# Queries projected once from packed weights and doubled when they leave PSUM, with two of four stacks and an output bias moved into the first batch

## The chip, the cores and the metric

The kernel runs on one core of a Trainium2 chip. The metric is device time in microseconds: the median of three executions was 816.04 us (814.54 to 821.61). All operands are float32. A product that needs full precision is made in one of two ways: as a plain float32 matmul, or as three matmuls on operands split into a rounded high part and a remainder (`_hi`, `_lo`, type float32r).

## The reference, cut to what matters

x is (8, 64, 256), so 512 tokens, and the context is (8, 1024, 256). Six layers follow each other, each of them `x = x + layer(layernorm(x))`. The change touches the first one only:

```python
q = split_heads(query @ w_q.T + b_q)          # query = layernorm(x); 16 heads of 16
k = split_heads(key @ w_k.T + b_k)            # key = value = ctx_1024
v = split_heads(value @ w_v.T + b_v)
scores = jnp.einsum('bhqd,bhkd->bhqk', q, k) / scale
attn = jax.nn.softmax(scores, axis=-1)
ctx = jnp.einsum('bhqk,bhkd->bhqd', attn, v)
out = ctx.transpose(0, 2, 1, 3).reshape(B, -1, D_MODEL) @ w_o.T + b_o
```

After it come an S4 filter over the batch axis, a mixture of 16 experts, a masked attention on the same context, a state-space layer, and a mixture of 9 experts.

## The kernel before, in words

Each engine has its own stream of instructions, written by hand in `build`; the streams meet only at semaphores. An engine runs its stream strictly in order, so a wait in it holds up everything behind it.

**The first layer.** The normalized tokens are transposed into `xnT` (features on partitions). Queries are kept in four stacks g = 0 to 3 of 64 features (`STACKS`). To make up for the split of the keys into a high and a low half, which share the 128 partitions of `k_stack`, every query feature must stand twice, on partitions 0 to 63 and again on 64 to 127. Before the change this doubling is done on the host: `wq` in the tile `first` has each group of 64 columns twice (512 columns per half of the input), and `bq` likewise. TensorE makes four products of 128 x 512 (L1882), ScalarE adds the bias and rounds each into `q_hi` (L1019), VectorE makes the remainder `q_lo` (L1315), and GpSimd spreads both over four masked copies for one batch element, `q_stack_hi` and `q_stack_lo` (`split_heads`, L633, one pair of operations for each stack).

**Batches.** Eight batch elements follow, `batch(b, ...)` on TensorE, ScalarE and VectorE, each of eight steps i. Step i takes the scores of two heads-groups (stack g = i // 2) against 1024 keys, and beside them makes one piece of keys or values: pieces of this batch's second half of the keys at i = 0 and 2, values at i = 1, 3, 5, 7, and at i = 4 and 6 the first half of the keys of the **next** batch element. VectorE takes the maximum of the scores (L1376, L1379), and then copies out the piece (`key_piece` L1324, `value_piece` L1335) and the first half of the previous step's transposed probabilities (L1348). ScalarE takes the exponential (L995), the high parts of keys (L982), the other half of the transposes (L1008), and at i = 1 the high part of the next context, `ctx_hi` (L974). GpSimd makes the low part, `ctx_lo` (`context_low`, L650, two operations of 128 x 1024). TensorE may start a key piece of the next batch only when both of those are done: `pe.wait_ge(ctx_lo_ready, DC * b + DC)` in `project_keys`.

**GpSimd's stream.** It is written out at L800 to L829, and near the change it reads:

```python
context_low(0, 0, range(1))
split_heads(0)
taps_parts = filter_taps()
next(taps_parts)
context_low(1, 1)
diagonals(0, 0)
split_heads(1)
```

`filter_taps` is a generator that holds the arithmetic of the S4 filter, cut in parts that are placed between the work of the attention. Its first part is 13 small operations (L660, the tiles `s_wr` to `s_g`).

**PSUM.** Before the change the queries use banks 2, 3, 5 and 6 (`Q_BANKS`), and the first two key pieces banks 4 and 7 (`FIRST_BANKS`). Bank 7 later holds the weighted values (`weigh`).

Of the kernel before, what the change touches and what calls it, by code (L numbers as in the profile page):

```python
# [20 lines left out]
P = 128  # L21
# [35 lines left out]
SPLIT1_AT = {GROUPS * m + g: 3 * (m - 1) + (g - 1) // 2 for m in (1, 2) for g in (1, 3, 5)}  # L57
LAYERS = 6

Q_BANKS, FIRST_BANKS = (2, 3, 5, 6), (4, 7)  # L60

# [49 lines left out]
def part(tile, layout, name):  # L113
    a, b = layout[name]
    return tile[:, a:b]
# [29 lines left out]
def build(nc, d, out):  # L145
    ctx = ExitStack()
    with ctx:
# [11 lines left out]
        def sb(region, name, shape, dt=F32):  # L159
            width = int(np.prod(shape[1:])) * 4  # L160
            at = place[region]
            place[region] = at + -(-width // 64) * 64
            assert place[region] <= ends[region], (name, region, place[region] - ends[region])
            return nc.alloc_sbuf_tensor_at(name, shape, dt, offset=at)
# [36 lines left out]
        w_kv = [[sb("phase", f"w_{n}_{part_of}", [P, DC, D], F32R) for part_of in ("hi", "lo")] for n in "kv"]  # L201
        k_stack = sb("phase", "k_stack", [P, STACKS, KEYS], F32R)
        V = sb("phase", "V", [P, KC, D])
        probs = [sb("phase", f"probs{k}", [P, KEYS]) for k in range(2)]
        probsT = [sb("phase", f"probsT{k}", [P, KC, PAIRS, P]) for k in range(DC)]
        q_part = [sb("phase", f"q_{n}", [P, STACKS, TOK], F32R) for n in ("hi", "lo")]
# [174 lines left out]
        def pb(i):  # L381
            return banks[:, i, :] if isinstance(i, int) else banks[:, bass.ds(i, 1), :].rearrange("p a n -> p (a n)")
# [43 lines left out]
        w2_hi_ready, w2_lo_ready, w2_before = w_hi_ready, w_lo_ready, 2 - 2 * PLAIN  # L426
        share_ready, spread_ready, spread_turned, spreadT_ready = inverted, diag_ready, spread_taken, masked_ready
        share_before = DC * B
        last_taken, last_before = q_done, STACKS
        up_done, gelu_done, down_done = sem("up_done"), sem("gelu_done"), sem("down_done")  # L430

        mask_loaded = sem("mask_loaded")
# [59 lines left out]
        def norm_of(k, t):  # L492

            return TC * (k - 1) + t + 1
# [462 lines left out]
        def _(act):  # L957
# [56 lines left out]
                    .then_inc(w_hi_ready, 1)  # L1014
            transposed(1)
            context_high(0, 0)
            for g in range(STACKS):
                act.wait_ge(q_done, g + 1)
                nc.scalar.activation(q_part[0][:, g, :], pb(Q_BANKS[g]), ACT.Identity, bias=part(first, FIRST, "bq")[:, g:g + 1])\  # L1019
                    .then_inc(q_hi_ready, 1)  # L1020
            for half in range(2):
                key_piece(half + 1, 0, half, FIRST_BANKS[half])

            act.wait_ge(loaded["later"], 16)
            nc.scalar.activation(s4dt[:], part(later, LATER, "log_dt"), ACT.Exp).then_inc(s4_exp, 1)
# [236 lines left out]
        def _(dve):  # L1262
# [41 lines left out]

            dve.wait_ge(loaded["x"], 16)
            layer_norm(1)
            transposed(1)

            dve.wait_ge(ctx_hi_ready, DC)
            nc.vector.tensor_tensor(ctx_lo[0][:, 1, :], ctx_raw[:, 1, :], ctx_hi[0][:, 1, :].bitcast(F32), ALU.subtract).then_inc(ctx_lo_ready, 1)  # L1310
            bq, bk, bv = part(first, FIRST, "bq"), part(first, FIRST, "bk"), part(rows, ROWS, "bv")
            dve.wait_ge(loaded["first"], 16)
            for g in range(STACKS):
                dve.wait_ge(q_hi_ready, g + 1)
                nc.vector.scalar_tensor_tensor(q_part[1][:, g, :], pb(Q_BANKS[g]), bq[:, g:g + 1], q_part[0][:, g, :].bitcast(F32),  # L1315
                                               ALU.add, ALU.subtract).then_inc(q_lo_ready, 1)

            def key_piece(k_piece, c, half, bank=4):

# [52 lines left out]
            def batch(b, par, last, tile=None):  # L1372
                later_one = not (isinstance(b, int) and b == 0)
                for i in range(8):
                    dve.wait_ge(scores_done, 8 * b + (i + 1))
                    nc.vector.tensor_reduce(negmax_raw[i % 2][:], two(i % 2),  # L1376
                                            AX.X, ALU.max, negate=True).then_inc(raw_max, 1)
                    dve.wait_ge(raw_max, 8 * b + (i + 1))
                    nc.vector.tensor_scalar(negmax[i % 2][:], negmax_raw[i % 2][:], 0.25, None, ALU.mult)\  # L1379
                        .then_inc(max_ready, 1)  # L1380
                    if i in KEYS_AT:
                        key_piece(4 * b + 3 + KEYS_AT.index(i), 1, KEYS_AT.index(i))
                    elif i in VALUES_AT:
                        value_piece(piece_at(b, i, last), b, VALUES_AT.index(i))
                    elif i in NEXT_KEYS_AT and not last:
                        key_piece(4 * b + 5 + NEXT_KEYS_AT.index(i), 0, NEXT_KEYS_AT.index(i))
                    if i == 5 and tile is not None:
                        add_tile(tile)
                    if i == 4:
                        invert_sums(b, 0)  # L1390
                    if i == 0 and later_one:
                        invert_sums(b - 1, 1)
                    if i == 0 and later_one:
                        gather(b - 1, 1 - par, 0)
                    if i == 4 and later_one:
                        gather(b - 1, 1 - par, 1)
                    if i >= 1:
                        first_half(b, i - 1)
                    elif later_one:
                        first_half(b - 1, 7)  # L1400

                    if last and 1 <= i < TC:
                        dve.wait_ge(tile_added, i + 1)
                        norm_begin(2, i - 1)
                    if last and 5 <= i < TC + 4:
                        norm_tile(2, i - 5)
# [1 line left out]
            for half in range(2):  # L1408
                key_piece(half + 1, 0, half, FIRST_BANKS[half])
            dve.wait_ge(loaded["rows"], 16)  # L1410
            dve.wait_ge(xn_ready, norm_of(1, TC - 1))
            nc.vector.tensor_tensor(X[:], X[:], over(part(rows, ROWS, "bo"), TC, 1), ALU.add).then_inc(tile_added, 1)
            batch(0, 0, False)
            dve.wait_ge(s4_norm, 1)
            nc.vector.reciprocal(s4g[2][:], s4g[2][:]).then_inc(s4_norm, 1)
# [436 lines left out]
        def _(pe):  # L1852
# [23 lines left out]
            transpose_tokens(1)  # L1876
            keep_running(4, 1, table[:, 0:512])
            pe.wait_ge(loaded["first"], 16)
            wq = weights(first, FIRST, "wq", DC)
            pe.wait_ge(xt0_ready, 1)  # L1880
            pe.wait_ge(xt1_ready, 1)
            for g in range(STACKS):  # L1882
                for i in range(DC):
                    last = mm(pb(Q_BANKS[g]), wq[:, i, g * P:(g + 1) * P], xnT[:, i, :], i == 0, i == DC - 1)
                last.then_inc(q_done, 1)

            def three(o, a, b):
# [37 lines left out]
            def weigh(b, c, q):  # L1925

                pe.wait_ge(piece_taken, piece_at(b, VALUES_AT[q], isinstance(b, int) and b == B - 1))
                if q == 0:  # L1930
                    pe.wait_ge(pt0_ready, 8 * b + PAIRS * (c + 1))
                    pe.wait_ge(pt1_ready, 8 * b + PAIRS * (c + 1))
                    pe.wait_ge(diag_ready, DC * b + (c + 1))
                    if not (isinstance(b, int) and b == 0 and c == 0):
                        pe.wait_ge(masked_ready, DC * b + c)

                    for j in range(PAIRS):
                        mm(pb(7)[PAIR_W * j:PAIR_W * (j + 1), P:2 * P], part(table, TABLE, "pick"), inv_diag[:, j, :], True, True)
                for kc in (2 * q, 2 * q + 1):
                    for j in range(PAIRS):  # L1940
                        at = c * P + PAIR_W * j
                        last = mm(pb(7)[PAIR_W * j:PAIR_W * (j + 1), 0:P], V[:, kc, at:at + PAIR_W],
                                  probsT[c][:, kc, j, :], kc == 0, kc == KC - 1)
                last.then_inc(quarter_done, 1)
# [572 lines left out]
```

## Time and profile before

| what | value |
|---|---|
| median of three executions | 816.04 us |
| the profiled execution, its own time | 815.67 us |
| its span from first to last instruction | 813.8 us |
| TensorE busy | 719.9 us, 88% of the span |
| VectorE busy | 585.6 us, 72% |
| GpSimd busy | 430.5 us, 53% |
| ScalarE busy | 417.8 us, 51% |
| mean granted TensorE clock | 0.968 of full |

An engine's busy share is a mean over six very different layers; the change lies in the first 60 us, so that part has to be read by itself. In the timelines a row is a group of instructions that follow each other: its start, its length, and in brackets how long the engine was idle before it and what ended that idle time. PE is TensorE, DVE VectorE, ACT ScalarE, POOL GpSimd. A float32 matmul stands in the trace as two instructions.

### The profile page before, as it was taken

Reading aid. Unit: us, or ns where it says so; the run is one execution under the profiler, and the core shown is the slowest. Engines: PE = TensorE matmul, PEld = TensorE weight load, DVE = VectorE, ACT = ScalarE, POOL = GpSimd, SP = SyncE. Lnnn points to the kernel's source line nnn. Section 1 sums busy time; section 2 is a strip of 40 time slices with the busy share of each in tenths; the row PEclk is TensorE's granted clock in tenths of the full one; section 3 lists DMA queues with packets and bytes.
Section 4 is the critical chain, followed back from the end, with each engine's and each line's share of the span. In section 5 each row is a group of like instructions: output and inputs, shape, how many; then the busy total and the mean of one; then the engine's idle time right before and its main releaser. Section 6 shows DMA issues by size and latency. Waiting matters only on the chain.

```text
span 813.8 us, 14674 instructions
## 1 busy us (share of the span) xinstructions
PE 719.9 (88%) x5252; PEld 562.6 (69%) x5252; DVE 585.6 (72%) x1210; ACT 417.8 (51%) x777; POOL 430.5 (53%) x417
## 2 busy tenths in 40 slices
PE   7899999999999997699999999999887776776886
PEld 3677777777777786599999999985463222222676
DVE  4788777887877857307777777715564999998585
ACT  3666656665665533146666666532337554432331
POOL 4637344363542712657878777556122879864130
PEclk9999999999999997899999999999999789989999
DMA  8011010010102049598989989988533700001000
GB/s 341 25 47 54 2 53 27 24 52 0 52 0 98 7 178 412 210 362 323 420 324 343 341 336 344 341 325 352 207 117 139 297 0 0 1 0 39 1 0 27
DMA packets 21225, 126.60 MB, mean 156 GB/s; under 512 B 2304, under 2 KB 6800, under 8 KB 13872
## 3 DMA queue, kind: packets, MB, share of 16 engines
q1 hardware_dynamic: 18288, 118.00, 38.3%
q0 software_dynamic: 2880, 7.87, 2.6%
q8 instruction: 32, 0.52, 0.3%
q14 instruction: 25, 0.20, 0.1%
HBM read 115.04 MB, written 10.81 MB: 155 GB/s over the span
## 4 chain that ended last, share of the span: by engine, by line
PE 57%; DVE 17%; POOL 10%; issue 8%; ACT 5%; DMA 2%; DVEq 0%; SPq 0%; ACTq 0%; POOLq 0%; PEldq 0%
PE banks L1854 51%; DVE banks L1760 6%; PE banks L1921 4%; DVE k_stack L1324 3%; POOL inject L924 3%; POOL y_rows L878 2%; ACT k_stack L982 1%; DVE negmax_raw L1376 1%; ACT ctx_hi L974 1%; DMA first<-in_first 1%; POOL f_lo L944 1%; DMA y_slots<-y_tile 1%; POOL rstd L622 1%; DVE shown L1770 1%; PE banks L2089 1%
## 5 line engine op out<-in xcount | busy, mean ns | idle before, releaser
L1854 PE MATMUL banks<-xT,raw 128*128 128x128 f32 x992 | 150.9, 275 | 2.3 <-issue 0.9
L1854 PEld LDWEIGHTS banks<-xT,raw 128*128 128x128 f32 x992 | 134.4, 191 | 6.1 <-issue 2.7
L858 POOL TENSOR_TENSOR w_lo<-raw,w_hi 128x1024 fp32r<-128x1024 f32 x48 | 113.2, 2379 | 1.9 <-ACT w_hi L1067 1.0
L1854 PE MATMUL banks<-shown,table 128*128 128x512 f32 x128 | 72.5, 697 | 42.2 <-DVE shown L1770 35.5
L995 ACT ACTIVATE probs<-banks,negmax 128x1024 f32<-128x1024 f32 x64 | 71.4, 1116 | 58.6 <-DVE negmax L1379 57.9
L924 POOL TENSOR_TENSOR inject<-BCbc,drive 128x1024 f32<-128x1024 f32 x32 | 75.0, 2352 | 36.4 <-DVE banks L1760 21.0
L1098 ACT ACTIVATE banks<-banks,later 128x128 f32<-128x128 f32 x192 | 65.2, 340 | 53.5 <-PE banks L1854 52.3
L1376 DVE TENSOR_REDUCE negmax_raw<-banks 128x1 f32<-128x1024 f32 x64 | 78.0, 1219 | 19.6 <-PE banks L1854 19.5
L1854 PEld LDWEIGHTS banks<-shown,table 128*128 128x128 f32 x128 | 24.6, 212 | 86.5 <-DVE shown L1770 67.6
L1588 DVE CAST mid_hi<-banks 128x128 fp32r<-128x128 f32 x192 | 55.5, 289 | 32.9 <-ACT banks L1098 30.6
L1760 DVE TENSOR_TENSOR_SCAN banks<-banks,inject 128x1024 f32<-128x1024 f32 x32 | 73.2, 2288 | 3.3 <-POOL inject L924 3.3
L1210 ACT ACTIVATE banks<-delta,exp_a 128x512 f32<-128x512 f32 x64 | 41.6, 682 | 62.2 <-DVE shown L1770 61.6
L1921 PE MATMUL banks<-table,probs 128*128 128x128 f32 x512 | 70.1, 280 | 0.0
L1854 PE MATMUL banks<-w_hi,mid_hi 128*128 128x256 f32 x192 | 69.7, 363 | 0.0
L982 ACT ACTIVATE k_stack<-banks,first 64x512 fp32r<-64x512 f32 x64 | 43.6, 681 | 42.8 <-PE banks L1854 41.9
L643 POOL TENSOR_TENSOR inv_diag<-table,inv_sums 128x512 f32<-128x512 f32 x16 | 16.6, 1040 | 91.4 <-DVE inv_sums L1342 54.9
L1324 DVE SCALAR_TENSOR_TENSOR k_stack<-banks,first,k_stack 64x512 fp32r<-64x512 f32 x64 | 48.0, 750 | 23.4 <-ACT k_stack L982 22.9
L1921 PEld LDWEIGHTS banks<-table,probs 128*128 128x128 f32 x512 | 55.9, 142 | 11.9 <-issue 11.3
L1590 DVE TENSOR_TENSOR mid_lo<-banks,mid_hi 128x128 fp32r<-128x128 f32 x192 | 56.0, 292 | 6.6
L1854 PE MATMUL banks<-k_stack,q_stack_hi 128*128 128x512 f32 x128 | 55.9, 436 | 0.0
L1854 PE MATMUL banks<-w_hi,mid_lo 128*128 128x256 f32 x192 | 54.0, 281 | 0.0
L1854 PE MATMUL banks<-w_lo,mid_hi 128*128 128x256 f32 x192 | 54.0, 281 | 0.0
(315 smaller groups left out, 1753.8 us busy)
## 6 DMA issues: line engine op xcount, KB each, us to landing
raw<-in_w SPq DMA_DIRECT2D x31, 2048.0 KB, 8.5
ctx_raw<-in_ctxT SPq DMA_DIRECT2D x8, 1024.0 KB, 4.8
ctxT<-in_ctxT SPq DMA_DIRECT2D x4, 2048.0 KB, 12.1
ctxN<-in_ctxN SPq DMA_DIRECT2D x4, 2048.0 KB, 12.4
BCbc<-bc_rows SPq DMA_DIRECT2D x6, 1024.0 KB, 14.2
x_slots<-zero SPq DMA_DIRECT2D x1, 3968.0 KB, 12.1
y_slots<-y_tile POOLq DMA_DIRECT2D x28, 128.0 KB, 6.9
wf<-in_w SPq DMA_DIRECT2D x9, 384.0 KB, 5.8
```

The costliest lines, as they stand in the source:

```text
L858: nc.gpsimd.tensor_tensor(w2_lo[i % WB][:, cols], raw[i % WB][:, EW // 2:][:, cols], w2_hi[i % 2][:, cols].bitcast(F32), ALU.subtract).the ...
L924: nc.gpsimd.tensor_tensor(inject[g % 2][:], Bbc[:, GS * g:GS * (g + 1), :], over(drive[:, m, :], GS, 1), ALU.mult).then_inc(inject_ready, 1)
L982: nc.scalar.activation(k_stack[at, DC * c + g, half * 512:(half + 1) * 512], pb(bank)[at, :], ACT.Identity, bias=part(first, FIRST, "bk")[ ...
L995: nc.scalar.activation(probs[i % 2][:], two(i % 2), ACT.Exp, bias=negmax[i % 2][:], scale=0.25, accum_out=sums[i // PAIRS][:, i % PAIRS:i ...
L1098: nc.scalar.activation(to, held, ACT.Gelu, bias=b1[:, bass.ds(at + u, 1)]).then_inc(gelu_done, 1)
L1324: last = nc.vector.scalar_tensor_tensor(k_stack[to, DC * c + g, cols], pb(bank)[at, :], bk[at, c:c + 1], k_stack[at, DC * c + g, cols].bit ...
L1376: nc.vector.tensor_reduce(negmax_raw[i % 2][:], two(i % 2), AX.X, ALU.max, negate=True).then_inc(raw_max, 1)
L1588: nc.vector.tensor_copy(mid_hi[n % HB][:], held).then_inc(mid_hi_ready, 1)
L1590: nc.vector.tensor_tensor(mid_lo[n % HB][:], held, mid_hi[n % HB][:].bitcast(F32), ALU.subtract).then_inc(mid_lo_ready, 1)
L1760: nc.vector.tensor_tensor_scan(held, held, inject[g % 2][:].rearrange("p g n -> p (g n)"), 0.0, ALU.mult, ALU.add).then_inc(scanned, 1)
L1854: return nc.tensor.matmul(o, lhsT, rhs, start=start, stop=stop)
L1921: last = nc.tensor.transpose(pb(5 + half)[:, k * P:(k + 1) * P], probs[i % 2][:, kc * P:(kc + 1) * P], ident)
```

## The change

- VectorE packs `wq` into a new tile `wq_dense` without the doubled columns (one copy, between the layer norm and its copy of `xnT`), and TensorE multiplies from it: two products of 128 x 512 in place of four. `Q_BANKS` is now (2, 7) and `FIRST_BANKS` (4, 3).
- The doubling happens as the queries leave PSUM: for each stack ScalarE makes two operations on 64 partitions (`query_high`), and VectorE two (`query_low`).
- Stacks 0 and 1 (`EARLY_Q`) are taken where all four were taken before. On ScalarE stacks 2 and 3 come behind the first two key pieces. On VectorE stack 2 comes in step 1 and stack 3 in step 2 of the first batch.
- The output bias, one addition to `X` on VectorE ahead of the first batch, now lies in step 3 of the first batch.
- `weigh` of the first batch also waits for all four `q_lo`, since bank 7 held queries. GpSimd's stream has the same instructions in the same order.

```diff
-Q_BANKS, FIRST_BANKS = (2, 3, 5, 6), (4, 7)
+Q_BANKS, FIRST_BANKS = (2, 7), (4, 3)
+EARLY_Q = 2
...
+        wq_dense = nc.alloc_sbuf_tensor_at("wq_dense", [P, DC, D], F32, offset=place["phase"])
...
-            for g in range(STACKS):
-                act.wait_ge(q_done, g + 1)
-                nc.scalar.activation(q_part[0][:, g, :], pb(Q_BANKS[g]), ACT.Identity, bias=part(first, FIRST, "bq")[:, g:g + 1])\
-                    .then_inc(q_hi_ready, 1)
+            bq = part(first, FIRST, "bq")
+
+            def query_high(g):
+                c, at = g // 2, slice(64 * (g % 2), 64 * (g % 2) + 64)
+                act.wait_ge(q_done, c + 1)
+                for z in range(2):
+                    last = nc.scalar.activation(q_part[0][64 * z:64 * z + 64, g, :], pb(Q_BANKS[c])[at, :], ACT.Identity, bias=bq[at, g:g + 1])
+                last.then_inc(q_hi_ready, 1)
+
+            for g in range(EARLY_Q):
+                query_high(g)
             for half in range(2):
                 key_piece(half + 1, 0, half, FIRST_BANKS[half])
+            for g in range(EARLY_Q, STACKS):
+                query_high(g)
...
             layer_norm(1)
+            dve.wait_ge(loaded["first"], 16)
+            order.mark(nc.vector.tensor_copy(wq_dense[:].rearrange("p c (g n) -> p c g n", g=STACKS),
+                                             part(first, FIRST, "wq").rearrange("p (c g n) -> p c g n", c=DC, g=STACKS)[:, :, :, 0:64]))
             transposed(1)
...
-            for g in range(STACKS):
+
+            def query_low(g):
+                c, at = g // 2, slice(64 * (g % 2), 64 * (g % 2) + 64)
                 dve.wait_ge(q_hi_ready, g + 1)
-                nc.vector.scalar_tensor_tensor(q_part[1][:, g, :], pb(Q_BANKS[g]), bq[:, g:g + 1], q_part[0][:, g, :].bitcast(F32),
-                                               ALU.add, ALU.subtract).then_inc(q_lo_ready, 1)
+                for z in range(2):
+                    last = nc.vector.scalar_tensor_tensor(q_part[1][64 * z:64 * z + 64, g, :], pb(Q_BANKS[c])[at, :], bq[at, g:g + 1],
+                                                          q_part[0][at, g, :].bitcast(F32), ALU.add, ALU.subtract)
+                last.then_inc(q_lo_ready, 1)
...
+                    if not later_one and 0 < i <= STACKS - EARLY_Q:
+                        query_low(EARLY_Q + i - 1)
+                    if not later_one and i == STACKS - EARLY_Q + 1:
+                        add_out_bias()
...
             dve.wait_ge(loaded["rows"], 16)
-            dve.wait_ge(xn_ready, norm_of(1, TC - 1))
-            nc.vector.tensor_tensor(X[:], X[:], over(part(rows, ROWS, "bo"), TC, 1), ALU.add).then_inc(tile_added, 1)
             batch(0, 0, False)
...
-            wq = weights(first, FIRST, "wq", DC)
+            pe.wait_ge(dve_step, 1)
             pe.wait_ge(xt0_ready, 1)
             pe.wait_ge(xt1_ready, 1)
-            for g in range(STACKS):
+            for c in range(DC):
                 for i in range(DC):
-                    last = mm(pb(Q_BANKS[g]), wq[:, i, g * P:(g + 1) * P], xnT[:, i, :], i == 0, i == DC - 1)
+                    last = mm(pb(Q_BANKS[c]), wq_dense[:, i, c * P:(c + 1) * P], xnT[:, i, :], i == 0, i == DC - 1)
                 last.then_inc(q_done, 1)
...
-                    if not (isinstance(b, int) and b == 0 and c == 0):
+                    if isinstance(b, int) and b == 0 and c == 0:
+                        pe.wait_ge(q_lo_ready, STACKS)
+                    else:
                         pe.wait_ge(masked_ready, DC * b + c)
```

VectorE's stream before, from the queries' low parts to step 2 of the first batch (a name's trailing number tells buffers apart, "waits" names the semaphores):

```order
L1315 SCALAR_TENSOR_TENSOR q_lo<-banks,first,q_hi 128x512 [waits q_hi_ready,loaded_first]
L1315 SCALAR_TENSOR_TENSOR q_lo<-banks,first,q_hi 128x512 [waits q_hi_ready] x3
L1324 SCALAR_TENSOR_TENSOR k_stack<-banks,first,k_stack 64x512 [waits k_hi_ready] x4
L1412 TENSOR_TENSOR X<-X,rows 128x1024 [waits xn_ready,loaded_rows]
L1376 TENSOR_REDUCE negmax_raw_88<-banks 128x1 [waits scores_done]
...
L1335 TENSOR_TENSOR V<-banks,rows 128x512 [waits proj_done]
L1348 COPY probsT_82<-banks 128x4x128 [waits t_done]
L1376 TENSOR_REDUCE negmax_raw_88<-banks 128x1 [waits scores_done]
L1379 TENSOR_SCALAR negmax_90<-negmax_raw_88 128x1 [waits raw_max]
L1324 SCALAR_TENSOR_TENSOR k_stack<-banks,first,k_stack 64x512 [waits k_hi_ready] x2
L1348 COPY probsT_82<-banks 128x4x128 [waits t_done]
```

The same stretch of VectorE's stream now:

```order
L1332 SCALAR_TENSOR_TENSOR q_lo<-banks,first,q_hi 64x512 [waits q_hi_ready,loaded_first]
...
L1349 SCALAR_TENSOR_TENSOR k_stack<-banks,first,k_stack 64x512 [waits k_hi_ready] x4
L1401 TENSOR_REDUCE negmax_raw_89<-banks 128x1 [waits scores_done]
...
L1360 TENSOR_TENSOR V<-banks,rows 128x512 [waits proj_done]
L1332 SCALAR_TENSOR_TENSOR q_lo<-banks,first,q_hi 64x512 [waits q_hi_ready]
L1332 SCALAR_TENSOR_TENSOR q_lo<-banks,first,q_hi 64x512
L1373 COPY probsT_83<-banks 128x4x128 [waits t_done]
...
L1349 SCALAR_TENSOR_TENSOR k_stack<-banks,first,k_stack 64x512 [waits k_hi_ready] x2
L1332 SCALAR_TENSOR_TENSOR q_lo<-banks,first,q_hi 64x512 [waits q_hi_ready]
L1332 SCALAR_TENSOR_TENSOR q_lo<-banks,first,q_hi 64x512
L1373 COPY probsT_83<-banks 128x4x128 [waits t_done]
```

Four operations on `q_lo` stand ahead of the first key pieces, two behind the values of step 1, two behind the key piece of step 2; the addition to `X` is gone from ahead of the first maximum.

GpSimd's stream now, which differs from before in its line numbers alone, from the third stack of `split_heads(0)` to the next context's low part:

```order
L635 TENSOR_TENSOR q_stack_hi<-q_hi,table 128x256 [waits q_lo_ready]
L635 TENSOR_TENSOR q_stack_lo<-q_lo,table 128x256
L635 TENSOR_TENSOR q_stack_hi<-q_hi,table 128x256 [waits q_lo_ready]
L635 TENSOR_TENSOR q_stack_lo<-q_lo,table 128x256
L662 TENSOR_TENSOR s_wr<-s_ew,s_dt 128x32 [waits loaded_later,s4_exp]
...
L662 TENSOR_TENSOR s_g_107<-s_g_107,s_g_108 128x160 [waits pool_step]
L652 TENSOR_TENSOR ctx_lo_72<-ctx_raw,ctx_hi_71 128x1024 [waits pool_step,ctx_hi_ready]
L652 TENSOR_TENSOR ctx_lo_72<-ctx_raw,ctx_hi_71 128x1024 [waits ctx_hi_ready]
```

Nothing moved here, but the second wait for `q_lo_ready` in it is for an operation that VectorE now issues in step 2 of the first batch.

## Rows read from the trace of the kernel before

**Rows 1.** The page: busy time by engine, and the chain's shares by engine
```profile
PE 719.9 (88%) x5252; PEld 562.6 (69%) x5252; DVE 585.6 (72%) x1210; ACT 417.8 (51%) x777; POOL 430.5 (53%) x417
PE 57%; DVE 17%; POOL 10%; issue 8%; ACT 5%; DMA 2%; DVEq 0%; SPq 0%; ACTq 0%; POOLq 0%; PEldq 0%
```

**Rows 2.** The chain of work in order of time, first 76 us: start, length, what
```profile
1.79 7.89 DMA first<-in_first
...
11.43 8.51 PE banks L1854 x22
...
41.84 0.69 ACT k_stack L982
...
68.59 4.75 POOL ctx_lo L650 x2
73.47 2.23 PE banks L1854 x22
```

**Rows 3.** Timeline of PE, 10 to 62 us
```profile
11.43 7.10 PE L1854 MATMUL banks<-xnT,first 128*128 128x512 f32 x16 [0.56 <-ACT xnT L960]
17.98 0.80 PE L1854 MATMUL banks<-ctx_hi,w_k_hi 128*128 128x512 f32 x1
...
28.10 0.39 PE L1854 MATMUL banks<-w_v_hi,ctx_hi 128*128 128x256 f32 x1 [2.13 <-DVE k_stack L1324]
...
31.98 0.47 PE L1854 MATMUL banks<-k_stack,q_stack_hi 128*128 128x512 f32 x1
...
36.92 0.39 PE L1854 MATMUL banks<-w_v_hi,ctx_hi 128*128 128x256 f32 x1 [0.59 <-DVE k_stack L1324]
...
39.26 0.47 PE L1854 MATMUL banks<-k_stack,q_stack_hi 128*128 128x512 f32 x1
...
40.26 0.39 PE L1854 MATMUL banks<-ctx_hi,w_k_hi 128*128 128x512 f32 x1
```

**Rows 4.** Windows: busy us (instructions) of PE, PEld, DVE, ACT, POOL, granted clock, DMA
```profile
29.00:30.00 1.00, 1.00 (x7) 1.00 (x7) 0.46 (x2) 0.48 (x1) 0.84 (x3) 0.50 0.00 0
```

**Rows 5.** Timeline of DVE, 8 to 42 us
```profile
9.21 0.69 DVE L1296 COPY xnT<-banks 128x512 f32<-128x512 f32 x1 [0.78 <-PE banks L1868]
14.26 2.54 DVE L1310 TENSOR_TENSOR ctx_lo<-ctx_raw,ctx_hi 128x1024 fp32r<-128x1024 f32 x1 [4.37 <-ACT ctx_hi L974]
...
20.68 3.06 DVE L1324 SCALAR_TENSOR_TENSOR k_stack<-banks,first,k_stack 64x512 fp32r<-64x512 f32 x4 [0.63 <-ACT k_stack L982]
23.77 1.23 DVE L1412 TENSOR_TENSOR X<-X,rows 128x1024 f32<-128x1024 f32 x1
...
30.87 0.69 DVE L1335 TENSOR_TENSOR V<-banks,rows 128x512 f32<-128x512 f32 x1 [1.38 <-PE banks L1854]
...
35.36 1.51 DVE L1324 SCALAR_TENSOR_TENSOR k_stack<-banks,first,k_stack 64x512 fp32r<-64x512 f32 x2 [0.75 <-ACT k_stack L982]
```

**Rows 6.** Timeline of ACT, 8 to 36 us
```profile
10.76 0.58 ACT L960 ACTIVATE xnT<-banks 128x512 f32<-128x512 f32 x1
...
19.97 2.81 ACT L982 ACTIVATE k_stack<-banks,first 64x512 fp32r<-64x512 f32 x4 [0.70 <-PE banks L1854]
...
34.65 1.38 ACT L982 ACTIVATE k_stack<-banks,first 64x512 fp32r<-64x512 f32 x2
```

**Rows 7.** Timeline of POOL, 20 to 39 us
```profile
21.54 0.61 POOL L633 TENSOR_TENSOR q_stack_lo<-q_lo,table 128x256 fp32r<-128x256 f32 x1
23.20 0.24 POOL L660 TENSOR_TENSOR s_wr<-s_ew,s_dt 128x32 f32<-128x32 f32 x1 [1.05 <-ACT s_ew L1026]
...
23.84 1.48 POOL L660 TENSOR_TENSOR s_g<-s_wr,table 128x160 f32<-128x160 f32 x1
25.39 0.46 POOL L660 TENSOR_TENSOR s_g<-s_wi,table 128x160 f32<-128x160 f32 x1
...
30.32 0.52 POOL L660 TENSOR_TENSOR s_g<-s_g,s_g 128x160 f32<-128x160 f32 x1
33.89 4.74 POOL L650 TENSOR_TENSOR ctx_lo<-ctx_raw,ctx_hi 128x1024 fp32r<-128x1024 f32 x2 [3.04 <-ACT ctx_hi L974]
```

More of the change, by code:

```diff
@@ L428, in build @@
         share_before = DC * B
-        last_taken, last_before = q_done, STACKS
+        last_taken, last_before = q_done, DC
         up_done, gelu_done, down_done = sem("up_done"), sem("gelu_done"), sem("down_done")
@@ L1312, in _, with add_out_bias @@
             dve.wait_ge(loaded["first"], 16)
-            for g in range(STACKS):
+            def query_low(g):
+                c, at = g // 2, slice(64 * (g % 2), 64 * (g % 2) + 64)
                 dve.wait_ge(q_hi_ready, g + 1)
-                nc.vector.scalar_tensor_tensor(q_part[1][:, g, :], pb(Q_BANKS[g]), bq[:, g:g + 1], q_part[0][:, g, :].bitcast(F32),
-                                               ALU.add, ALU.subtract).then_inc(q_lo_ready, 1)
+                for z in range(2):
+                    last = nc.vector.scalar_tensor_tensor(q_part[1][64 * z:64 * z + 64, g, :], pb(Q_BANKS[c])[at, :], bq[at, g:g + 1],
+                                                          q_part[0][at, g, :].bitcast(F32), ALU.add, ALU.subtract)
+                last.then_inc(q_lo_ready, 1)
+            def add_out_bias():
+                dve.wait_ge(xn_ready, norm_of(1, TC - 1))
+                nc.vector.tensor_tensor(X[:], X[:], over(part(rows, ROWS, "bo"), TC, 1), ALU.add).then_inc(tile_added, 1)
+            for g in range(EARLY_Q):
+                query_low(g)
             def key_piece(k_piece, c, half, bank=4):
```

## The prediction

> **What bounds the kernel now.** I read the page first. TensorE is busy 88% of the span and VectorE 72% [rows 1], but that is a mean over six layers, and the change touches 60 us. So the second view is the chain of waits in order of time. In the first 76 us it runs from a transfer over TensorE's queries to the high and low copies of the keys and back, and then over GpSimd: `ctx_lo` holds TensorE up at 73.47 [rows 2]. The reader should see two things. The key piece of the next batch element, whose copy by ScalarE stands at 41.84, is on the chain; and GpSimd, busy only 53% of the time, is on it wherever `ctx_lo` comes late. The third view is the timeline of each engine, 8 to 42 us, from which I rebuild the schedule.
>
> TensorE's queries take 7.10 us for 16 instructions, and the first keys follow at 17.98, though `ctx_lo` had been ready since 16.80 [rows 3, 5]. That is the delay the change aims at. GpSimd, in its own stream, finishes the fourth stack of query copies at 22.15, does the first part of the filter from 23.20 to 30.84, waits 3.04 us, and makes the next context's low part from 33.89 to 38.63 [rows 7]. TensorE first needs that at 40.26 [rows 3], in step 4 of the first batch. Slack: 1.63 us. This small number decides the case.
>
> **The change, part by part.**
>
> *Packing.* `first` lands at 1.79 + 7.89 = 9.68 [rows 2]. A copy of 128 x 512 costs at most the 0.69 us of the `xnT` copy [rows 5], at least nothing. VectorE's `xnT` then ends by 9.68 + 0.69 + 0.69 = 11.06, and ScalarE's half ends at 11.34 [rows 6], so TensorE still starts at 11.43. Price 0, cover 0.28 us, and the worst case costs less than that again.
>
> *Queries on TensorE.* Eight instructions for 16: 3.55 us less, done at 14.98. The keys now wait for `ctx_lo`, 16.80, and start about 16.9: gain 1.08 of the 3.55 us.
>
> *Copies, lead-in.* A key copy of 64 x 512 is the nearest row: 3.06 / 4 = 0.765 us on VectorE, 2.81 / 4 = 0.70 us on ScalarE [rows 5, 6]. Half the partitions save nothing against 0.69 us for 128 x 512. ScalarE fits the two early stacks (2.8 us from 14.13) in before the first keys are ready, 19.97 - 1.08 = 18.89. VectorE goes from 16.80 over four low parts to 19.86 and over four key copies to 22.92, where it was 23.74: 0.82 us gained. Taking away the addition to `X` (1.23 us at 23.77) gains nothing here, as it lay under TensorE's first scores.
>
> *ScalarE behind the keys.* 18.89 + 2.81 + 4 x 0.70 for stacks 2 and 3 = 24.50; two small exponentials (0.34) and the next key copies (2 x 0.70) end at 26.24. VectorE's last copy of that piece then ends at 27.22 against 28.04, so TensorE's values start at 27.28 against 28.10 [rows 3]. The 0.82 us are still there, which is what the change looks like up to this point.
>
> *VectorE inside the batch.* Values are copied at 30.05 to 30.74, stack 2 then takes 1.53 us to 32.27. The transposes' copy (0.69) and the next maximum (1.42 with its scaling) end at 34.38, still under the wait for ScalarE's key copy, whose first half is ready at 34.65 - 0.82 + 0.69 = 34.52. The key pair of step 2 ends at 36.05, and the low part of **stack 3 ends at 37.6**.
>
> *GpSimd behind it.* Its stream has the spreading of stack 3 ahead of the filter's part, and that ahead of the next `ctx_lo`. So everything queued there now starts after 37.6 where the spreading had been finished at 22.15. Stack 3: 1.2 us, to 38.85. The filter's part: 30.84 - 23.20 = 7.64 us, to 46.55. `ctx_lo`: 4.74 us, to 51.35 [rows 7]. TensorE starts 0.14 us after such an end (73.34 to 73.47 [rows 2]), at 51.5. Before: 40.26. **Step 4 is 11.2 us late.** TensorE, whose stream stands at that wait, holds back the keys that ScalarE and VectorE wait for in the same step.
>
> In those 7.64 us one operation took 1.48 us, its like 0.46, and the long one ran while VectorE added to `X` (23.77 to 25.00) [rows 5, 7]. The moved addition comes in step 3, at about 40.3, again over the filter's part, so I keep the 1.48; without a meeting 1.0 us would be saved. The Trainium skill, page "SBUF — State Buffer", section "Who interferes with whom", says that a VectorE operation with two SBUF inputs and a GpSimd operation that reads SBUF exclude each other for a whole instruction. By that rule the sum stays as it is, by the other reading it is 1.0 us smaller; the trace agrees with the rule.
>
> *The clock.* After 2.13 us of idle TensorE's clock was granted at 0.50, its lower level, 1.2 GHz [rows 4]. A value piece and a turn took 31.98 - 28.10 = 3.88 us, where the same pair at full clock takes 39.26 - 36.92 = 2.34 [rows 3]: 1.54 us lost. A wait of some 9 us at step 4 will do no less, and the keys behind it are on the chain: 1.5 us, bounds 0 and 2.7 (twelve key matmuls at half speed). The Trainium skill, page "TensorE: Matmul & The Clock Gate", part 1, has the clock at half after an idle stretch until the engine has been busy again. Without that rule's loss the sum would be 11.2, with it 12.7; the trace shows the loss after the shorter idle.
>
> *Later.* Nothing gives the time back. The transfers (`ctx_raw`, the experts) are started by semaphores of this same stream, so they move along. In the next batch the chain already goes through GpSimd (`ctx_lo` 68.59 [rows 2]), behind values that now come later too. The addition to `X` in step 3 (1.23 us) and the new wait before `weigh` (satisfied from 37.6, asked for after 55) lie under the stall; if the stall were not there, the addition and the two `q_lo` pairs would cost about 1 us net at step 4 (1.53 + 1.53 + 1.23 us of VectorE work, less what lies under its waits and the 0.82 gained).
>
> **Sum.** 815.67 + 11.2 + 1.5 = 828.4 for the profiled execution; its time is 0.37 below the median, so 828.5 to 828.7. I forecast **828.5 us**. This kernel tells about 1% (8.2 us) from no change.
>
> **The rivals.**
> 1. *GpSimd's delay stays hidden.* The profile speaks for it at first sight: GpSimd idles 3.04 us before `ctx_lo` and 53% is a low share. It decides at one point: the low part of stack 3 would have to end by 40.26 - 0.14 - 13.6 = 26.5, and it ends 11 us later. Should I have misread that dependency, VectorE's extra work shows alone: about 817, within 1%. Chance 8%.
> 2. *Not slower: the lead-in gain comes through.* The place is TensorE's start on the keys; its price is 0.8 to 3.5 us (813 to 815), and it needs both GpSimd's work in time and VectorE's extra 3 us covered by its waits. Against it: TensorE can't start before `ctx_lo` at 16.80. Chance 3%; only with something unseen would it reach 1% (1%).
> 3. *The queue on GpSimd and a lower clock already at the start.* TensorE now idles from 14.98 to 16.9; if the clock falls there, the twelve matmuls of the first two pieces take up to 2.7 us more, and stack 3 comes as much later: about 831. Chance 12%.
> The forecast itself: 77%.
>
> **Range.** Down: no meeting with the addition (-1.0), no half clock after the stall (-1.5) nor on the first values (-1.0): 825; the shown runs of one kernel lie up to 1.5 below their median, so 823.5. Up: rival 3 and half a microsecond: 832. Rivals 1 and 2 lie outside. Slower by over 1% means over 824.2: 0.88. Faster by over 1%: 0.01. Within: 0.11.
>
> **What would show it.** Right: in the timeline of the changed kernel TensorE's queries have 8 instructions ending about 15; keys start about 16.9; the last `q_lo` ends about 37.6; GpSimd runs without a gap from there to about 51; TensorE is idle about 42 to 51, released by GpSimd's `ctx_lo`, with a granted clock near 0.5 behind it; from then on every row is later by the same 12 to 13 us. Wrong: `ctx_lo` of the second batch ending before 41, or a difference at step 4 that shrinks in later batches or in the expert layer.

## The result: 1.7% slower, and what the profile shows after

The changed kernel takes **830.48 us** (median of 4 runs, 829.92 to 835.26) against 815.84 us (median of 4, 814.54 to 821.61) for the kernel before beside it: ratio **1.0174 [1.0142, 1.0205]**, 14.6 us more. The forecast was 828.5 us, between 823.5 and 832.

The page of the changed kernel first: busy time by engine, then the chain's shares by engine.

```profile
PE 720.7 (87%) x5244; PEld 565.0 (68%) x5244; DVE 589.1 (71%) x1215; ACT 421.3 (51%) x781; POOL 430.9 (52%) x417
PE 55%; DVE 17%; POOL 12%; issue 9%; ACT 5%; DMA 3%; DVEq 0%; SPq 0%; ACTq 0%; POOLq 0%; PEldq 0%
```

Against [rows 1] hardly a busy time moved: TensorE has 8 instructions fewer and 0.8 us more, VectorE 3.5 us more. Whoever reads the page alone finds no 14 us. On the chain GpSimd's share grew from 10% to 12% of the span, with the same 417 instructions: not more work, but work that others now wait for. (The shares of `issue` and DMA grew by one point each, TensorE's fell by two.)

The chain of waits of the changed kernel, in order of time (start, length, what):

```profile
2.27 9.04 DMA ctx_raw<-in_ctxT
...
28.96 0.65 DVE q_lo L1332
...
30.45 0.61 POOL q_stack_hi L635
...
36.67 0.61 POOL q_stack_hi L635
37.29 0.57 POOL q_stack_lo L635
38.45 0.47 POOL s_g L662
...
44.78 0.53 POOL s_g L662
45.48 4.65 POOL ctx_lo L652 x2
50.17 2.93 PE banks L1881 x6
...
80.13 4.75 POOL ctx_lo L652 x2
85.00 2.20 PE banks L1881 x22
```

Before, GpSimd was not on the chain until 60.49 (`inv_diag`, and behind it filter operations up to the `ctx_lo` of 68.59), and the key copy of 41.84 was [rows 2]. Now GpSimd's whole queue from 36.67 to 50.13 is on it. And the `ctx_lo` of the next batch element comes 11.5 us later, 80.13 for 68.59.

GpSimd's timeline in the changed kernel (start us, us, engine, line, operation, out<-in, shape, count, idle time before it and its releaser):

```profile
30.45 0.61 POOL L635 TENSOR_TENSOR q_stack_hi<-q_hi,table 128x256 fp32r<-128x256 f32 x1 [10.32 <-DVE q_lo L1332]
31.03 0.62 POOL L635 TENSOR_TENSOR q_stack_lo<-q_lo,table 128x256 fp32r<-128x256 f32 x1
36.67 0.61 POOL L635 TENSOR_TENSOR q_stack_hi<-q_hi,table 128x256 fp32r<-128x256 f32 x1 [5.03 <-DVE q_lo L1332]
...
37.81 0.24 POOL L662 TENSOR_TENSOR s_wr<-s_ew,s_dt 128x32 f32<-128x32 f32 x1
...
39.52 1.38 POOL L662 TENSOR_TENSOR s_g<-s_g,s_g 128x160 f32<-128x160 f32 x1
...
42.58 0.52 POOL L662 TENSOR_TENSOR s_g<-s_g,s_g 128x160 f32<-128x160 f32 x1
...
45.48 4.64 POOL L652 TENSOR_TENSOR ctx_lo<-ctx_raw,ctx_hi 128x1024 fp32r<-128x1024 f32 x2 [0.18 <-POOL s_g L662]
```

The filter part that began at 23.20 [rows 7] begins at 37.81. GpSimd idles 10.32 and 5.03 us for a `q_lo` each time, and from 36.67 on it works with next to no gap.

VectorE, whose `q_lo` of stacks 2 and 3 release those waits:

```profile
15.82 3.05 DVE L1332 SCALAR_TENSOR_TENSOR q_lo<-banks,first,q_hi 64x512 fp32r<-64x512 f32 x4
...
28.88 1.49 DVE L1332 SCALAR_TENSOR_TENSOR q_lo<-banks,first,q_hi 64x512 fp32r<-64x512 f32 x2
...
35.07 1.52 DVE L1332 SCALAR_TENSOR_TENSOR q_lo<-banks,first,q_hi 64x512 fp32r<-64x512 f32 x2
...
39.15 1.37 DVE L1338 TENSOR_TENSOR X<-X,rows 128x1024 f32<-128x1024 f32 x1
53.86 1.51 DVE L1349 SCALAR_TENSOR_TENSOR k_stack<-banks,first,k_stack 64x512 fp32r<-64x512 f32 x2 [11.41 <-ACT k_stack L984]
```

The last of these rows is VectorE's key copy of step 4. Before it stood here:

```profile
42.55 1.51 DVE L1324 SCALAR_TENSOR_TENSOR k_stack<-banks,first,k_stack 64x512 fp32r<-64x512 f32 x2 [0.69 <-ACT k_stack L982]
```

It is 11.3 us later now, after 11.41 us of idleness. The row names ScalarE as releaser; ScalarE itself waited for TensorE's keys. TensorE's timeline:

```profile
10.95 3.60 PE L1881 MATMUL banks<-xnT,wq_dense 128*128 128x512 f32 x8
...
16.04 0.47 PE L1881 MATMUL banks<-ctx_hi,w_k_hi 128*128 128x512 f32 x1 [1.49 <-DVE ctx_lo L1324]
...
26.38 0.39 PE L1881 MATMUL banks<-w_v_hi,ctx_hi 128*128 128x256 f32 x1 [2.22 <-DVE k_stack L1349]
...
50.17 0.80 PE L1881 MATMUL banks<-ctx_hi,w_k_hi 128*128 128x512 f32 x1 [10.71 <-POOL ctx_lo L652]
...
55.74 0.28 PE L1881 MATMUL banks<-w_v_hi,ctx_hi 128*128 128x256 f32 x1
```

Queries are halved, and the keys start earlier (16.04 for 17.98), as do the values (26.38 for 28.10) [rows 3]; 0.86 us of each is that `first` landed earlier in this execution (8.82 for 9.68). Then one wait of 10.71 us, released by GpSimd's `ctx_lo`. And the windows over it (busy us and instructions of PE, PEld, DVE, ACT, POOL, granted clock, DMA share, GB/s):

```profile
40.00:45.00 5.00, 0.00 (x0) 0.00 (x0) 2.41 (x4) 0.37 (x1) 4.37 (x9) 0.64 0.00 0
45.00:50.00 5.00, 0.00 (x0) 0.00 (x0) 0.00 (x0) 0.00 (x0) 4.82 (x3) 0.50 0.00 0
50.00:55.00 5.00, 4.83 (x15) 4.08 (x16) 1.13 (x2) 1.81 (x3) 0.12 (x1) 0.50 0.61 210
55.00:60.00 5.00, 5.00 (x53) 4.33 (x52) 3.82 (x7) 3.06 (x6) 4.34 (x7) 0.99 0.00 0
```

TensorE does nothing for 10 us, and from 42.4 on GpSimd alone works; in the idle stretch the granted clock falls to 0.50, the level of 1.2 GHz, and stays there for the first 5 us of work.

### The profile page after: what moved, and what is told of

Read it like the earlier page. It is cut to its first block, busy times and chain, and to the rows that moved or that the text cites. A ratio compares the mean times of both kernels' runs of the same rounds, so it can differ in the third digit from the quotient of the medians.

```text
span 828.1 us, 14668 instructions
## 1 busy us (share of the span) xinstructions
PE 720.7 (87%) x5244; PEld 565.0 (68%) x5244; DVE 589.1 (71%) x1215; ACT 421.3 (51%) x781; POOL 430.9 (52%) x417
## 4 chain that ended last, share of the span: by engine, by line
PE 55%; DVE 17%; POOL 12%; issue 9%; ACT 5%; DMA 3%; DVEq 0%; SPq 0%; ACTq 0%; POOLq 0%; PEldq 0%
PE banks L1881 49%; DVE banks L1787 6%; PE banks L1948 4%; POOL inject L926 3%; DVE k_stack L1349 2%; POOL y_rows L880 2%; DVE negmax_raw L1401 1%; ACT k_stack L984 1%; POOL ctx_lo L652 1%; DMA ctx_raw<-in_ctxT 1%; ACT ctx_hi L976 1%; POOL f_lo L946 1%; POOL s_g L662 1%; DMA y_slots<-y_tile 1%; POOL rstd L624 1%
## 5 line engine op out<-in xcount | busy, mean ns | idle before, releaser
L1948 PEld LDWEIGHTS banks<-table,probs 128*128 128x128 f32 x512 | 56.8, 144 | 12.8 <-issue 12.2
```

Source lines behind the costliest of these rows:

```text
L1948: last = nc.tensor.transpose(pb(5 + half)[:, k * P:(k + 1) * P], probs[i % 2][:, kc * P:(kc + 1) * P], ident)
```

## The experiments

The theory: stack 3's low part, late on VectorE, holds up GpSimd's stream, that holds up `ctx_lo`, and that holds up TensorE. The rivals: TensorE's new pauses and clock; the doubled number of small copies; the moved addition to `X`. Each ratio is against runs of the kernel before on the same chip. Those had medians of 808.11, 821.61 and 820.09 us on the three chips used, so times of different groups are not compared, only ratios.

**1. Only GpSimd's order.** The changed kernel, with stacks 2 and 3 spread where their data is ready, around the filter part and `ctx_lo`.

```diff
-            split_heads(0)
+            split_heads(0, (0, 1))
...
             next(taps_parts)
+            split_heads(0, (2,))
             context_low(1, 1)
+            split_heads(0, (3,))
```

> The changed kernel, with GpSimd's stream alone put in another order: stacks 0 and 1, the filter's first part, stack 2, the next context's low part, and only then stack 3. Theory (the wait for the late stack 3 stands ahead of the filter's part and ctx_lo): the filter's part runs about 24 to 31, ctx_lo 33 to 37, TensorE starts the next keys in step 4 at about 40 with no wait for ctx_lo, its clock stays up, and the time falls from 830.5 by 12 to 14 us to 816 to 818. Rival (the extra copies on VectorE and ScalarE and the moved addition make the loss): they are all still there, so it stays above 826.

Measured: 808.78 us, ratio 1.0016 [0.999, 1.0041]. GpSimd in this run:

```profile
24.39 0.24 POOL L662 TENSOR_TENSOR s_wr<-s_ew,s_dt 128x32 f32<-128x32 f32 x1 [3.61 <-ACT s_ew L1039]
...
32.52 4.73 POOL L652 TENSOR_TENSOR ctx_lo<-ctx_raw,ctx_hi 128x1024 fp32r<-128x1024 f32 x2
37.30 0.61 POOL L635 TENSOR_TENSOR q_stack_hi<-q_hi,table 128x256 fp32r<-128x256 f32 x1
```

and TensorE:

```profile
40.01 0.47 PE L1883 MATMUL banks<-ctx_hi,w_k_hi 128*128 128x512 f32 x1
```

No wait ahead of the keys, and they stand at 40.01 for 40.26 [rows 3]. All other work of the change (half-size copies, packing, moved addition, pause before the first keys) is still in it. VectorE's key copy of step 4 comes at 42.95 for 42.55, straight behind other work of VectorE, so this work costs 0.4 us there, and by the interval at most 3.3 us in the whole. This is shown: with stack 3 as late as in the changed kernel (`q_lo` at 35.70), the order of GpSimd's queue alone decides on the loss.

**2. The reverse: one operation moved in the kernel before.** Everything stays as before, and only the low part of stack 3, one operation of 0.75 us on VectorE, goes to step 2 (with it, banks 6 and 7 swap roles, and the first `weigh` waits for it).

```diff
-Q_BANKS, FIRST_BANKS = (2, 3, 5, 6), (4, 7)
+Q_BANKS, FIRST_BANKS = (2, 3, 5, 7), (4, 6)
...
+            for g in range(STACKS - 1):
+                query_low(g)
...
+                    if not later_one and i == 2:
+                        query_low(STACKS - 1)
...
+                    if isinstance(b, int) and b == 0 and c == 0:
+                        pe.wait_ge(q_lo_ready, STACKS)
```

> The kernel before, its doubled weights and four products included, with one VectorE operation moved: the low part of stack 3 (128 x 512, 0.7 us) goes from ahead of the first key copies to step 2 of the first batch; bank 7 holds its queries, so FIRST_BANKS is (4, 6) and weigh waits for it as in the change. Theory: GpSimd's queue is held till 37.6 as in the changed kernel, the next ctx_lo ends at 51.2, and with the half clock behind the wait the time is 12.4 us over before: about 828. Rival (the loss needs the doubled copies): 816, as one operation of 0.7 us changes place.

Measured: 823.71 us, ratio 1.0191 [1.0149, 1.0233]. GpSimd:

```profile
37.69 0.61 POOL L633 TENSOR_TENSOR q_stack_hi<-q_hi,table 128x256 fp32r<-128x256 f32 x1 [17.72 <-DVE q_lo L1315]
...
38.83 0.24 POOL L660 TENSOR_TENSOR s_wr<-s_ew,s_dt 128x32 f32<-128x32 f32 x1
...
45.62 4.63 POOL L650 TENSOR_TENSOR ctx_lo<-ctx_raw,ctx_hi 128x1024 fp32r<-128x1024 f32 x2 [0.18 <-POOL s_g L660]
```

The key copy of step 4 comes at 53.99 for 42.55, 11.4 us late. One small operation, none added, reproduces the whole loss: the half-size copies, the packing and the moved addition are not in this kernel. The 15.6 us measured are more than the 12.4 expected, as with the changed kernel itself; more on that below. Here the addition to `X` is in its old place and meets no filter operation: the part takes 6.6 us (38.83 to 45.44) where it takes 7.5 in the changed kernel.

**3. All four stacks early.** The changed kernel with its copies where they used to be (the addition to `X` then comes in step 1).

```diff
-EARLY_Q = 2
+EARLY_Q = 4
```

> The changed kernel with EARLY_Q = 4: the same doubled copies, but all four stacks ahead of the first keys, on VectorE and ScalarE (the addition to X then comes in step 1). Theory: GpSimd gets stack 3 at about 23 and has ctx_lo ready before step 4; what is left is the longer lead-in, 8 x 0.765 us of low parts before the key copies, end of these 26.0 for 23.7 before, so 2 us over the kernel before: about 818. Rival (doubling on the way out of PSUM is what costs, wherever it lies): 826 or more.

Measured: 812.09 us, ratio 1.0047 [1.0025, 1.0068], 4.0 us. VectorE:

```profile
16.02 6.14 DVE L1332 SCALAR_TENSOR_TENSOR q_lo<-banks,first,q_hi 64x512 fp32r<-64x512 f32 x8
22.19 3.06 DVE L1349 SCALAR_TENSOR_TENSOR k_stack<-banks,first,k_stack 64x512 fp32r<-64x512 f32 x4
```

Eight operations for four, 6.14 us, and the key copies start at 22.19 for 20.68 [rows 5]. At step 4 the kernel is 1.4 us late (43.97 for 42.55), or 2.1 us counted from the landing of `first`, which was 0.67 us earlier: about the 2 us expected. At 300 us it is still 1.4 us (the row of `by_tile`, 301.23 for 299.80). The other 2.6 us are not in this stage, and where they come from was not found; the interval reaches from 2.0 to 5.5 us. What is shown: nearly three quarters of the loss (14.6 to 4.0 us) vanish without touching GpSimd, once `q_lo` is there in time.

**4. A longer filter part.** If GpSimd's queue is the path, what is added to it there must show one for one. The changed kernel, with nine more operations in the filter part.

```diff
-                tt(g[2], g[0], g[0], mul)
-                tt(g[3], g[1], g[1], mul)
-                tt(g[2], g[2], g[3], add)
+                for _ in range(4):
+                    tt(g[2], g[0], g[0], mul)
+                    tt(g[3], g[1], g[1], mul)
+                    tt(g[2], g[2], g[3], add)
```

> The changed kernel, with the last three operations of the filter's first part made four times over (nine more of 128 x 160, 0.50 us from start to start, 4.5 us; the values stay the same). Theory: every microsecond in GpSimd's queue ahead of ctx_lo is one on the whole, the clock being down already: 835.0. Rival (TensorE waits at step 4 for something else, or the wait is made good later): 830.5 to 832.

Measured: 827.23 us, ratio 1.0234 [1.0195, 1.0273]: 19.1 us over the kernel before, where the change cost 14.6. `ctx_lo` starts at 50.34 for 45.48, and TensorE follows:

```profile
55.02 0.79 PE L1882 MATMUL banks<-ctx_hi,w_k_hi 128*128 128x512 f32 x1 [15.68 <-POOL ctx_lo L652]
```

4.86 us more work in the queue, 4.85 us later keys (55.02 for 50.17). The total agrees within its interval.

**5. TensorE kept running through the wait**, with eleven products that nobody reads, to price the clock alone.

```diff
+                    if isinstance(b, int) and b == 0 and i == NEXT_KEYS_AT[0]:
+                        pe.wait_ge(q_lo_ready, STACKS)
+                        keep_running(7, 11, table[:, 0:512])
```

> The changed kernel, with eleven plain float32 matmuls of 128 x 512 into bank 7 (a free bank there, their result isn't used) put in TensorE's stream at step 4 of the first batch, ahead of the next keys: they run in the wait for ctx_lo, 0.89 us each, 9.8 us of a wait of 11. Theory: the granted clock is still full when the keys start, the six key matmuls take 1.4 us and not 2.7, so the next steps come 1.4 to 1.7 us earlier than in the changed kernel: 1.0174 of before goes to about 1.0155. Rival (the clock costs nothing behind the wait, since something else ends last there): no difference at step 5.

**6. The changed kernel again**, on the same chip as 5.

> The changed kernel once more, beside the experiments on the same chip, for their difference to it. Ratio to before 1.017 as measured, 1.014 to 1.021.

Measured: 835.38 us, ratio 1.0135 [1.0094, 1.0176], for 5, and 833.99 us, ratio 1.0136 [1.009, 1.0182], for 6. TensorE and two windows in 5:

```profile
39.90 9.60 PE L1881 MATMUL banks<-table 128*128 128x512 f32 x22
50.80 0.50 PE L1881 MATMUL banks<-ctx_hi,w_k_hi 128*128 128x512 f32 x1 [1.29 <-POOL ctx_lo L652]
...
54.77 0.38 PE L1881 MATMUL banks<-w_v_hi,ctx_hi 128*128 128x256 f32 x1 [0.53 <-DVE k_stack L1349]
```

```profile
45.00:50.00 5.00, 4.50 (x11) 1.71 (x9) 0.00 (x0) 0.00 (x0) 4.74 (x4) 1.00 0.00 0
50.00:55.00 5.00, 3.68 (x20) 2.86 (x20) 1.72 (x4) 2.46 (x4) 0.74 (x1) 1.00 0.56 210
```

The clock stays at 1.00, and from the first key to the first value of step 5 it is 3.97 us (50.80 to 54.77), against 5.57 in the changed kernel, 5.25 in experiment 6 and 3.86 before (40.26 to 44.12). So the low clock costs 1.3 to 1.6 us at this place. Experiment 6 shows the wait again, 10.70 us, with the keys at 49.66. There the clock had stayed at 1.00 over the first values, stack 3's `q_lo` ended at 36.10 for 36.59 although `first` landed 0.81 us later, and at 300 us the kernel is 10.8 us behind the one before, where the changed kernel of the result is 11.7. In the total of four runs each, which lie 8 to 10 us apart among themselves, 1.5 us can't be seen, and they aren't.

**7. Only the addition to `X` moved**, in the kernel before.

```diff
+                    if not later_one and i == 3:
+                        dve.wait_ge(xn_ready, norm_of(1, TC - 1))
+                        nc.vector.tensor_tensor(X[:], X[:], over(part(rows, ROWS, "bo"), TC, 1), ALU.add).then_inc(tile_added, 1)
```

> The kernel before, with the addition of the output bias to X alone moved from ahead of the first batch to its step 3, as in the change. Theory: where it was it lay under TensorE's first scores, where it goes it stands ahead of the transposes' copy on VectorE, so 0 to 0.8 us more at step 4, and GpSimd's filter part is 1.0 us shorter in its old place: ratio to before 1.000 to 1.001. Rival (the moved addition makes a part of the loss): 1.003 or more.

Measured: 819.31 us, ratio 0.9967 [0.994, 0.9993]. It costs nothing, so it isn't the loss. At step 4 its trace has VectorE's key copy at 42.39, where two executions of the kernel before have 42.55 and 42.47; the 0.3% has no row that explains it.

**8. Another order, as a candidate.** In the kernel before, without packing or half-size copies: queries of stacks 0 to 2, two key pieces, then stack 3, on TensorE, ScalarE and VectorE alike; the addition to `X` in step 1.

```diff
-            for g in range(STACKS):
+            for g in range(STACKS - 1):
+                project_query(g)
...
+            project_query(STACKS - 1)
```

> The kernel before with its doubled weights and whole copies, and another order: TensorE makes stacks 0 to 2, the first two key pieces, then stack 3; ScalarE and VectorE copy stack 3 right behind those key pieces, ahead of the first batch, and the addition to X lies in VectorE's idle time of step 1. Theory: the keys start with ctx_lo at 16.9 and not 17.98, GpSimd gets stack 3 at about 24, early enough for ctx_lo at 38.6, so 0.6 to 1.1 us are gained at step 4 and kept: ratio 0.999. Rival (stack 3 late by any amount costs): over 1.005.

Measured: 817.51 us, ratio 0.9947 [0.9919, 0.9974]. In this trace the key copy of step 4 comes at 39.57, 2.9 us ahead of the kernel before; number 10 tells how much of that is the order.

**9 and 10. The kernel before against itself, and number 8 once more**, on a third chip.

> The kernel before itself, timed against itself in the same way as the others, and profiled on the same chip as the next run. Its ratio must hold 1.000; how far its median lies from 1 tells what the ratios 0.9967 and 0.9947 of the last two can be worth. If it lies at 1.000 within 0.2%, the two small gains stand as measured; if at 0.997, they are the measurement's.

> Stack 3 behind the keys once more, beside the kernel before on one chip. Theory: 0.6 to 1.1 us gained at step 4 against e0_before, measured from the landing of the tile first, and kept to the end, ratio 0.998 to 1.000; the 0.9947 of the last time holds more than that. Rival (the order gains 4 us, somewhere later): 0.995 again, and the traces differ by 3 us or more behind the first layer.

Measured: the kernel before 821.4 us, ratio 1.0007 [0.9979, 1.0036]; the candidate 817.76 us, ratio 0.9969 [0.9938, 1.0]. TensorE in the candidate, then in the kernel before on the same chip:

```profile
16.81 0.47 PE L1863 MATMUL banks<-ctx_hi,w_k_hi 128*128 128x512 f32 x1
```

```profile
17.95 0.79 PE L1854 MATMUL banks<-ctx_hi,w_k_hi 128*128 128x512 f32 x1
```

The keys start 1.14 us earlier, and at step 4 the lead is 1.17 us (VectorE's key copy 41.30 for 42.47; 0.08 us of it is an earlier landing of `first`). This is the gain that the change aimed at, had by order alone, and with GpSimd's queue fed in time. Of the 2.9 us in the trace of number 8, 1.5 us are not the order but the clock: there it stayed at 1.00 over the first values, here it was granted at 0.50, and from the first to the next values it is 7.26 us there (26.68 to 33.94) and 8.79 here (26.87 to 35.66). The end of the two traces can't be read for the gain: this one ends 6.3 us ahead of the kernel before on the same chip (816.3 for 822.6) and 2.5 us behind the execution of the result section (813.8), and most of these differences arise behind 345 us. The gain is 0.14% by the rows of the first layer, and 0.3% and 0.5% by the two timings: small, of one sign, and at the edge of what can be told. Experiment 7 was timed at 0.9967 with no gain in its trace, so the timings alone would not carry it. What carries it is the row that stands earlier. Against the changed kernel it is ahead by more than either interval.

## Why the prediction was right, and where not

**The slack and the queue: right.** The step on which all hung was that stack 3's `q_lo` ends long after 26.5, and that GpSimd does 13.6 us of queued work behind it. In this execution `first` landed 0.86 us earlier, and the transfer behind it, `ctx_raw`, 0.90 us; the 0.86 is to be added to the times from the first keys on. Forecast / measured with that: last `q_lo` ends 37.6 / 37.45; GpSimd's queue 13.75 / 13.45 us (36.67 to 50.12); keys of step 4 at 51.5 / 51.03. One length was read too short: TensorE was said to be idle from about 42, some 9 us, though its last work ahead of these keys would end near 40; it idled 10.71 us, from 39.46 on. No term of the sum used that length. The moved operation, the queue and the wait are shown by experiments 1, 2 and 4.

**Queries and packing: right.** 8 instructions, over at 14.55 for 14.98; here they followed directly on TensorE's earlier work on the tokens, which hangs on `X`, and `X` landed 0.54 us later in this execution (4.83 for 4.29). Keys at 16.90 (with the 0.86) for about 16.9. The packing copy took 0.42 us (bounds were 0 and 0.69) and lies under cover: VectorE then still waited 0.44 us for TensorE before its copy of `xnT`. Copies on 64 partitions took about 0.76 and 0.69 us a piece, the price of the nearest rows. The aside that without the stall the change would cost about 1 us at step 4 was in the right place too: experiment 1 has 0.4 us, 0.6 from the landing of `first`.

**The meeting of the addition and the filter: right in kind.** A filter operation took 1.38 us where its like took 0.52, while VectorE added to `X` (39.15 to 40.52); the addition itself took 1.37 for 1.23 [rows 5]. Experiment 2, which has no such meeting, has a part shorter by 0.9 us (the text had 1.0). The row shows it first; the Trainium skill, page "SBUF — State Buffer", section "Who interferes with whom", says that a VectorE operation with two SBUF inputs contends with a GpSimd operation that reads SBUF, and the trace agrees.

**The clock: right in size.** 1.5 us were taken; the way from the keys of step 4 to the values of step 5 took 5.57 for 3.86 us, 1.7 more, and experiment 5 buys 1.3 to 1.6 of it back. The mechanism is as the page "TensorE: Matmul & The Clock Gate" of the Trainium skill has it in part 1 (half clock until busy again), and the trace agrees: 0.50 in 45 to 55, 0.99 behind that.

**The constant shift: right to 618 us, and the total partly by luck.** The text said that from step 4 every row is later by the same 12 to 13 us. Measured are +11.3 at step 4, +11.5 at the next `ctx_lo`, +11.7 at 287 us (`tap_diag` 286.86 for 275.16), +11.8 at 356 us and +11.9 at 618 us, or 12.2 to 12.8 counted from the landing of `first`, where 12.7 was forecast. At 636 us it is +13.6, and +14.3 at the end (span 828.1 for 813.8). These rows of VectorE, of the kernel before and then of the changed one, show it:

```profile
344.54 0.42 DVE L1596 COPY y_tile<-banks 128x256 f32<-128x256 f32 x1 [11.57 <-remote]
...
606.05 8.02 DVE L1698 SCALAR_TENSOR_TENSOR conv_acc<-banks,later,conv_acc 128x244 f32<-128x244 f32 x18 [1.01 <-ACT a_pad L1147]
622.66 0.75 DVE L1721 TENSOR_SCALAR delta<-banks,later 128x512 f32<-128x512 f32 x1 [8.59 <-ACT drive L1183]
```

```profile
356.34 0.43 DVE L1623 COPY y_tile<-banks 128x256 f32<-128x256 f32 x1 [9.43 <-remote]
...
617.99 8.10 DVE L1725 SCALAR_TENSOR_TENSOR conv_acc<-banks,later,conv_acc 128x244 f32<-128x244 f32 x18 [1.01 <-ACT a_pad L1158]
636.29 0.75 DVE L1748 TENSOR_SCALAR delta<-banks,later 128x512 f32<-128x512 f32 x1 [10.20 <-ACT drive L1194]
```

So 2.4 of the 14.3 us come from no term of the sum and arise in code that the change doesn't touch. The larger piece, 1.7 us, lies between the last two rows: 18.30 us for 16.61, with TensorE's clock granted at 0.57 in 618 to 622 where the kernel before had 1.00. This isn't tied to the change, for both lengths occur in both kernels. The changed kernel in experiment 6 takes 16.61 us there, at 1.00, and the kernel before in experiment 9 takes 18.12, with 0.50 in 620.6 to 622.6. Without these 2.4 us the profiled execution would have taken some 827.5 us and not 829.92; both lie in the range, so the range holds without luck. That 828.5 and 830.48 lie so close is luck in part: the earlier landing of `first` took 0.86 us away, and 2.4 us came that were not foreseen.

How far executions of one program part is told by experiment 9: its trace agrees with that of the first execution to 0.1 us up to 312 us and to 0.2 us at 344.7, is 6.5 us behind at the `conv_acc` row, 8.05 at `delta`, and 8.8 at the end (spans 822.6 and 813.8). Of the totals, ratios of 1.0174, 1.0191 (experiment 2) and 1.0136 (experiment 6) stand beside local delays of 11.7, 11.9 and 10.8 us at 300 us, 1.3 to 1.5% of the time. How the rest of the first two, 2.9 and 3.7 us, splits between chance and the change was not settled.

**The rivals.** That GpSimd's delay stays hidden, and that the lead-in gain comes through, fell with the 10.71 us of wait; the lead-in gain itself was there (1.1 us at the keys) and was lost at step 4. That a low clock already stretches the first pieces fell on one row: the first key product takes 0.47 us, and the chain's ten products from 20.56 on take 2.71 us, the pace of full clock.

## What to carry to other kernels

- Before an operation is moved later, follow its result into every other engine's stream, and count all that is queued behind the wait there, related or not: here a result of 0.75 us (experiment 2; 1.52 us in the changed kernel) held up 13.5 us of GpSimd work, and the slack was 1.63 us.
- An engine's low busy share says nothing on its slack: GpSimd was busy 53% before and 52% after. What counts is when the last thing that it owes is ready, against when it is asked for.
- When work is taken later on one engine, take the order of its consumers along: a few lines in GpSimd's order turned 1.0174 into 1.0016.

## What the runs showed of the hardware

- The same program differs between chips and executions by more than this change's smaller terms: medians of the kernel before were 815.84, 808.11, 821.61 and 820.09 us in four groups of runs. One place shows much of it. In the expert layer, from the first `xT` to the first `y_tile`, the four kernels profiled on the chip of experiments 1 to 4 take 11.2 to 13.5 us, with DMA at 355 to 409 GB/s, and the eight profiled elsewhere 22.8 to 24.4 us, at 238 to 252 GB/s.
- The same idle time doesn't always bring the same clock. In two executions of one kernel (numbers 8 and 10) TensorE idled 2.14 and 2.15 us ahead of the first values. In the first the clock stayed at 1.00, in the second it was at 0.50 from 27 to 30 us, and from the first values to the next it took 7.26 and 8.79 us.
- Halving the partitions of a copy saves nothing: four operations of 64 x 512 on VectorE took 3.05 us, 0.76 each, where three whole ones of 128 x 512 of the same kind took 2.06 in the kernel before, 0.69 each, and one by itself 0.75 (experiment 2). Doubling on the way out of PSUM thus doubles the copies' time; with all of them ahead of the key copies (experiment 3) these start 1.5 us later.
- The granted clock fell in a stretch in which TensorE was idle but GpSimd busy, 0.64 in 40 to 45 us and 0.50 in 45 to 50; products that nobody reads held it at 1.00, and cost nothing in the trace but TensorE's own time.
